# A fused transformer stack on one core: the last attention's token weights as a row, and a new order of steps

## The reference

```python
Sim = (x @ w1)[:, :, None] + (ctx @ w2)[:, None, :] + einsum('bid,bjd->bij', x * w3, ctx) + b_sim
A = softmax(Sim, axis=2)
hq_hat = einsum('bij,bjd->bid', A, ctx)
Batt = softmax(max(Sim, axis=2), axis=1)          # one weight per token
hc_bar = einsum('bi,bid->bd', Batt, x)[:, None, :]
feats = concatenate([x, hq_hat, x * hq_hat, x * hc_bar], axis=-1)
out = feats @ W_qv + b_qv
```

## Time and profile before

| | us |
|---|---|
| median of 3 runs (3061.4 to 3073.03) | 3064.12 |
| the profiled execution's own time | 3070.26 |
| its span | 3068.5 |

### The profile page before, as it was taken

How to read it: one execution, slowest core, us unless ns; L and a number is a source line. 1 busy time by engine, 2 the same in 40 slices (tenths; PEclk the granted TensorE clock), 3 DMA queues, 4 the chain that set the end, 5 groups by cost and what they waited for, 6 DMA issues and landing times. The chain is left out here.

```text
span 3068.5 us, 78311 instructions
## 1 busy us (share of the span) xinstructions
PE 2755.7 (90%) x28313; PEld 1958.0 (64%) x28313; DVE 2595.8 (85%) x6995; ACT 2420.2 (79%) x6105; POOL 1027.2 (33%) x1693
## 2 busy tenths in 40 slices
PE   6999999999999669979999997976799999999997
PEld 4666666666666446657777775332667777777776
DVE  5899999999999426459999995798499999999996
ACT  3899989999999435547777774498499999999995
POOL 1344444444444200035555552000034444444441
PEclk8999999999999679989999997998899999999998
DMA  1012121111111021101111110000300000000000
GB/s 49 27 34 62 51 38 34 35 34 35 34 34 33 14 61 43 42 21 35 34 34 34 34 35 25 12 0 0 105 9 16 16 16 16 16 16 16 16 16 9
DMA packets 177630, 91.15 MB, mean 30 GB/s; under 512 B 46339, under 2 KB 174021, under 8 KB 177251
## 3 DMA queue, kind: packets, MB, share of 16 engines
q1 hardware_dynamic: 171716, 76.85, 9.3%
q0 software_dynamic: 4096, 8.40, 0.8%
q10 hardware_dynamic: 1440, 0.90, 0.1%
HBM read 43.73 MB, written 42.36 MB: 28 GB/s over the span
## 5 line engine op out<-in xcount | busy, mean ns | idle before, releaser
L2336 DVE TENSOR_TENSOR th<-tf 128x2048 f32<-128x2048 f32 (+1 forms) x256 | 574.1, 2243 | 6.6 <-ACT cg L2139 6.6
L2168 ACT ACTIVATE th<-th 128x2048 f32<-128x2048 f32 (+1 forms) x256 | 481.6, 1883 | 0.6 <-DVE th L2336 0.6
L652 ACT ACTIVATE probf<-probf,colf 128x128 f32<-128x128 f32 x1024 | 313.2, 393 | 0.0
L2116 POOL TENSOR_SCALAR colf<-colf 128x1 f32<-128x1 f32 x64 | 134.8, 2107 | 441.0 <-DVE colf L2317 441.0
L2230 PE MATMUL p_rho<-th,late_w_row 128*32 128x128 f32 x8064 | 277.5, 276 | 2.5 <-ACT th L2168 2.3
L2230 PEld LDWEIGHTS p_rho<-th,late_w_row 128*32 128x32 f32 x8064 | 209.3, 110 | 26.7 <-ACT th L2168 3.6
L1765 PE MATMUL acc<-xnT_all,wT 128*128 128x512 f32 x384 | 181.3, 625 | 29.6 <-DVE tmax L1957 13.2
L2179 ACT ACTIVATE tl<-tf 128x128 f32<-128x128 f32 x640 | 199.6, 391 | 0.0
L656 ACT COPY probTf<-fp 128x1024 f32<-128x1024 f32 x128 | 129.5, 1012 | 45.7 <-PE fp L800 45.7
L800 PE MATMUL fp<-ident,probf 128*128 128x128 f32 x1024 | 142.4, 284 | 23.6 <-ACT ygf L659 20.5
L747 PE MATMUL xp<-ident,prob 128*77 128x128 f32 x1024 | 142.3, 283 | 20.8 <-DVE colc L993 19.4
(11 more groups left out here) (437 smaller groups left out, 8543.1 us busy)
## 6 DMA issues: line engine op xcount, KB each, us to landing
rows<-zeros SPq DMA_DIRECT2D x64, 256.0 KB, 2.4
cxT<-in_ctxT SPq DMA_DIRECT2D x128, 38.5 KB, 1.9
xb<-rows SPq DMA_DIRECT2D x67, 64.0 KB, 1.8
rows<-yb SPq DMA_DIRECT2D x67, 64.0 KB, 1.5
x<-in_x SPq DMA_DIRECT2D x64, 64.0 KB, 1.8
x_mid<-x SPq DMA_DIRECT2D x64, 64.0 KB, 1.5
z<-x_mid SPq DMA_DIRECT2D x64, 64.0 KB
x_next<-z SPq DMA_DIRECT2D x64, 64.0 KB, 1.5
```

Source lines behind the costliest of these rows:

```text
L652: last = nc.scalar.activation(scores, scores, ACT.Exp, bias=colf[s][:, 16 + HALF * hf + h:17 + HALF * hf + h])
L2168: nc.scalar.activation(b, b, ACT.Tanh).then_inc(act_done, ACT_L.did(f"t{c}.tanh", e))
L2336: nc.vector.tensor_tensor(th[i % NT][:, 0:shape[1], :], tf[s][:, CHUNK[n]:CHUNK[n + 1]].unsqueeze(2).to_broadcast(shape), tf[s][:, FEAT:FE ...
```

## The change

x2.p is now one row of 128 exponents on one partition, with their sum behind it; x2.M gives the negated maximum at once, so x2.Mb and x2.negM are gone. x2.hq spreads the row and its sum over all partitions with one product of a row of ones (128 + 1 columns), and the product with the context stays. x2.hc multiplies the spread weights with the transposed tokens on VectorE, scales by the reciprocal and sums along the row into column 24. x2.out moves to columns 384 to 511 of `p_o`. All four orders of the pass are new.

```diff
 ACT_C, new:
+    x2.exp@4 x1.PT@1 x2.P@4 x2.PT@4 f1.uqT@3 x2.p@4 x2.kT@4 x1.xT f2.xT@5 f1.tanh@2 x2.feat@4 x1.qkv x2.xT@3 f1.xT@1
+    x1.exp f1.uround@2
 DVE_C, new:
+    f1.scale@2 x2.norm@4 f1.round@2 f1.silu@3 f1.xq@2 f1.uamax@3 f1.uclip@3 f1.urec@3 x1.max@1 f1.uscale@3 x2.x@5
+    x2.max@4 x1.z x2.score@4 x1.stats f2.stats@5 x2.rden@4 f1.uq@3 f2.aggr@5 x1.rden@1 x1.aggr x1.x@1 f2.amax@8
+    f1.stats@1 x2.M@4 f1.aggr@1 f2.norm@5 x1.norm f1.x@3 x2.stats@3 f1.norm@1 x2.aggr@3 f1.amax@1 x2.rsum@4 f1.inv@1
+    x2.hc@4 x2.ehq@4
 PE_C, new:
+    f1.tap1@2 f1.down@3 f2.T@5 x2.hq@4 x1.T f1.z@2 x1.qkv x2.T@3 x2.out@4 x1.S f1.T@1 x2.S@3 x1.PT f1.tap0@1 x1.y
+    f1.uqT@2 x2.PT@3
 POOL_C, new:
+    x2.eps@5 x2.rstd@5 in.gather f2.eps@6 x1.eps@1 f2.rstd@6 x1.rstd@1 f1.eps@2 f1.rstd@2
...
+        p_row = ring(NC, "p_row", [1, TOK + 1])
+        spent = sb("spent", [128, TOK])
...
-                act.wait_ge(dve_done, DVE_M.value("x2.negM", e))
-                nc.scalar.activation(col[s][:, 22:23], col[s][:, 19:20], ACT.Exp, bias=col[s][:, 21:22])...
+                act.wait_ge(dve_done, DVE_M.value("x2.M", e))
+                nc.scalar.activation(p_row[s][0:1, 0:TOK], p_s[0:1, 384:512], ACT.Exp, bias=col[s][0:1, 20:21], accum_out=p_row[s][0:1, TOK:TOK + 1])...
...
-                    pe.wait_ge(dve_done, DVE_M.value("x2.negM", e - 1))
+                    pe.wait_ge(act_done, ACT_M.value("x2.p", e - 1))
...
-                pe.wait_ge(dve_done, DVE_M.value("x2.M", e))
-                nc.tensor.matmul(p_s[:, 208:209], ones[0:1, :], col[s][0:1, 20:21], start=True, stop=True)...
...
-                nc.tensor.matmul(p_o[:, 128:129], xn[s][:], col[s][:, 22:23], start=True, stop=True)
-                nc.tensor.matmul(p_o[:, 130:131], ones[:], col[s][:, 22:23], start=True, stop=True)
+                nc.tensor.matmul(p_o[:, 128:129 + TOK], ones[0:1, :], p_row[s][:], start=True, stop=True)
...
-                nc.vector.tensor_reduce(c[0:1, 20:21], p_s[0:1, 384:512], X_AXIS, ALU.max)...
-                dve.wait_ge(pe_done, PE_M.value("x2.Mb", e))
-                nc.vector.tensor_scalar(c[:, 21:22], p_s[:, 208:209], -1.0, None, ALU.mult)...
+                nc.vector.tensor_reduce(c[0:1, 20:21], p_s[0:1, 384:512], X_AXIS, ALU.max, negate=True)...
...
-                nc.vector.reciprocal(c[:, 23:24], p_o[:, 130:131])...
+                nc.vector.reciprocal(c[:, 23:24], p_o[:, 128 + TOK:129 + TOK])...
...
-                nc.vector.tensor_scalar(c[:, 24:25], p_o[:, 128:129], c[:, 23:24], None, ALU.mult)...
+                nc.vector.scalar_tensor_tensor(spent[:], p_o[:, 128:128 + TOK], c[:, 23:24], xnT[s][:], ALU.mult, ALU.mult, accum_out=c[:, 24:25])...
```

More of the change, by code:

```diff
@@ L169 @@
 F2_BEHIND = 3
+PE_C = """
+    f1.tap1@2 f1.down@3 f2.T@5 x2.hq@4 x1.T f1.z@2 x1.qkv x2.T@3 x2.out@4 x1.S f1.T@1 x2.S@3 x1.PT f1.tap0@1 x1.y
+    f1.uqT@2 x2.PT@3
+"""
 ACT_C = """
-    x2.xT@4 x1.exp@1 x2.feat@5 f1.uround@3 x1.PT@1 x2.exp@4 x2.P@4 f1.uqT@3 x2.PT@4 x1.xT f2.xT@5 f1.tanh@2 x2.p@4
-    x1.qkv f1.xT@1 x2.kT@4
+    x2.exp@4 x1.PT@1 x2.P@4 x2.PT@4 f1.uqT@3 x2.p@4 x2.kT@4 x1.xT f2.xT@5 f1.tanh@2 x2.feat@4 x1.qkv x2.xT@3 f1.xT@1
+    x1.exp f1.uround@2
 """
 DVE_C = """
[L175 to L182, removed]
+    f1.scale@2 x2.norm@4 f1.round@2 f1.silu@3 f1.xq@2 f1.uamax@3 f1.uclip@3 f1.urec@3 x1.max@1 f1.uscale@3 x2.x@5
+    x2.max@4 x1.z x2.score@4 x1.stats f2.stats@5 x2.rden@4 f1.uq@3 f2.aggr@5 x1.rden@1 x1.aggr x1.x@1 f2.amax@8
+    f1.stats@1 x2.M@4 f1.aggr@1 f2.norm@5 x1.norm f1.x@3 x2.stats@3 f1.norm@1 x2.aggr@3 f1.amax@1 x2.rsum@4 f1.inv@1
+    x2.hc@4 x2.ehq@4
 """
 POOL_C = """
-    x1.rstd@3 f2.eps@8 f2.rstd@8 f1.eps@4 f1.rstd@4 x2.eps@6 x2.rstd@6 in.gather x1.eps@2
+    x2.eps@5 x2.rstd@5 in.gather f2.eps@6 x1.eps@1 f2.rstd@6 x1.rstd@1 f1.eps@2 f1.rstd@2
 """
@@ L1270, in x2 @@
                 yield
-                act.wait_ge(dve_done, DVE_M.value("x2.negM", e))
-                nc.scalar.activation(col[s][:, 22:23], col[s][:, 19:20], ACT.Exp, bias=col[s][:, 21:22]).then_inc(act_done, ACT_M.did("x2.p", e))
+                act.wait_ge(dve_done, DVE_M.value("x2.M", e))
+                nc.scalar.activation(p_row[s][0:1, 0:TOK], p_s[0:1, 384:512], ACT.Exp, bias=col[s][0:1, 20:21], accum_out=p_row[s][0:1, TOK:TOK + 1]).then_inc(act_done, ACT_M.did("x2.p", e))
                 yield
@@ L1394, in x2 @@
                 yield
-                pe.wait_ge(dve_done, DVE_M.value("x2.M", e))
-                nc.tensor.matmul(p_s[:, 208:209], ones[0:1, :], col[s][0:1, 20:21], start=True, stop=True).then_inc(pe_done, PE_M.did("x2.Mb", e))
-                yield
                 pe.wait_ge(act_done, ACT_M.value("x2.p", e))
@@ L1408, in x2 @@
                 for n, f in enumerate((xnT, kT, qT, yT)):
-                    nc.tensor.matmul(p_o[:, 256:256 + DIM], f[s][:], w_qv2[:, n, :], start=(n == 0), stop=False)
-                nc.tensor.matmul(p_o[:, 256:256 + DIM], ones_bf[:], row_bq, start=False, stop=True).then_inc(pe_done, PE_M.did("x2.out", e))
+                    nc.tensor.matmul(p_o[:, 384:384 + DIM], f[s][:], w_qv2[:, n, :], start=(n == 0), stop=False)
+                nc.tensor.matmul(p_o[:, 384:384 + DIM], ones_bf[:], row_bq, start=False, stop=True).then_inc(pe_done, PE_M.did("x2.out", e))
                 yield
@@ L1540, in x2 @@
                 dve.wait_ge(act_done, ACT_M.value("x2.PT", e))
-                nc.vector.tensor_reduce(c[0:1, 20:21], p_s[0:1, 384:512], X_AXIS, ALU.max).then_inc(dve_done, DVE_M.did("x2.M", e))
-                yield
-                dve.wait_ge(pe_done, PE_M.value("x2.Mb", e))
-                nc.vector.tensor_scalar(c[:, 21:22], p_s[:, 208:209], -1.0, None, ALU.mult).then_inc(dve_done, DVE_M.did("x2.negM", e))
+                nc.vector.tensor_reduce(c[0:1, 20:21], p_s[0:1, 384:512], X_AXIS, ALU.max, negate=True).then_inc(dve_done, DVE_M.did("x2.M", e))
                 yield
                 dve.wait_ge(act_done, ACT_M.value("x2.kT", e))
-                nc.vector.reciprocal(c[:, 23:24], p_o[:, 130:131]).then_inc(dve_done, DVE_M.did("x2.rsum", e))
+                nc.vector.reciprocal(c[:, 23:24], p_o[:, 128 + TOK:129 + TOK]).then_inc(dve_done, DVE_M.did("x2.rsum", e))
                 yield
                 after("x2.rsum", e)
-                nc.vector.tensor_scalar(c[:, 24:25], p_o[:, 128:129], c[:, 23:24], None, ALU.mult).then_inc(dve_done, DVE_M.did("x2.hc", e))
+                if e >= 1:
+                    after("x2.hc", e - 1)
+                nc.vector.scalar_tensor_tensor(spent[:], p_o[:, 128:128 + TOK], c[:, 23:24], xnT[s][:], ALU.mult, ALU.mult, accum_out=c[:, 24:25]).then_inc(dve_done, DVE_M.did("x2.hc", e))
                 yield
@@ L1554, in x2 @@
                 dve.wait_ge(pe_done, PE_M.value("x2.out", e))
-                nc.vector.tensor_tensor(z[s][:], p_o[:, 256:256 + DIM], z[s][:], ALU.add).then_inc(dve_done, DVE_M.did("x2.x", e))
+                nc.vector.tensor_tensor(z[s][:], p_o[:, 384:384 + DIM], z[s][:], ALU.add).then_inc(dve_done, DVE_M.did("x2.x", e))
                 yield
```

## The result

| | us |
|---|---|
| before, median of 6 runs | 3068.95 |
| changed, median of 6 runs (3082.67 to 3095.91) | 3085.94 |
| ratio, 95% interval | 1.0055 [1.0043, 1.0067] |
| forecast | 3072, range 3035 to 3096 |

The change made the kernel slower by 17 us. The forecast was 8 us slower, on a median of 3064.12 from the three runs of before that were known then: its direction was right, its size half of it. In the profiled executions the span went from 3068.5 to 3084.7.

A forecast was written before the change was run, and what follows sets the result against it. VectorE was taken to bound, with waits on ScalarE and GpSimd lengthening the turn from 8.42 to 8.56 us: +8.8 us over 63 turns, less 1 at the run-out, so +8 on 3064.12 gives 3072; range 3035 to 3096.

The forecast's parts named there:

- What bounds: VectorE sets the pace in the old second pass, by its work plus about 0.11 us per dependent neighbouring pair; turn 8.42.
- The chain through ScalarE: Two exponents around f1.uround delay x2.rden to 3.51 us after f1.silu, against 3.24 by VectorE's list: a wait of 0.27.
- The chain through GpSimd: GpSimd's eps and rstd steps delay the three norms by 0.46 us together; f1.norm at 6.66, x2.norm at 8.11.
- The next f1.silu at 8.56: End of the walked turn: f1.silu follows f1.round at 8.36, so a turn is 8.56 us against 8.42, +0.14.
- TensorE gets between 0.1 and 1.2 us back: Per turn, three products go and one single-partition product comes, taken to hold 0.22; 0.4 us saved, counted as slack.
- VectorE's +0.06 for the mean: Longer weighted mean with sum read-out, less two removed VectorE steps: net +0.05 to +0.13 us a turn, free in its gap.
- The round trip at the run-out: Removed maximum round trip through VectorE, TensorE and ScalarE counts once, at the last entry: 1 us gained, between 0 and 3.
- B: Rival, chance 0.13: TensorE's clock falls if its idle stretch behind x2.S reaches about 1 us; +48 us, about 3115.
- C: Rival, chance 0.10: sum read-out and single-partition product each cost 0.1 us beyond the slack; turn 8.7, time 3080.
- D: Rival, chance 0.18: the order matters little, the waits wander and the turn stays at 8.42 us; time 3063.
- A: Rival: shorter waits on ScalarE and GpSimd; mild, chance 0.13, turn 8.15, 3046; full, chance 0.08, turn 7.75, 3021.
- the signs of being wrong: Turn under 8.3, clock below 1.00 in mid-pass, or the last TensorE product, not GpSimd, releasing x2.norm's neighbours.

The follow-up runs named there:

- e8: New computation in the four orders of before, weighted mean over only 8 of 128 tokens, against the kernel before: ratio 0.9995, turn 8.47 us.
- e3: Changed kernel with the row of weights and its ones in bf16, making the spreading product one pass instead of two: ratio to before 1.0001, turn 8.51 us.
- e2: Changed kernel with the spreading product of x2.hq issued twice into the same place: ratio to before 1.0136, turn 8.98 us.
- e6: Computation of before, with x2.Mb, x2.negM and the short mean, put in the changed kernel's new orders: ratio to before 1.0169, turn 9.26 us.
- e5: Changed kernel with the weighted mean over only 8 of the 128 tokens: ratio to before 1.0055, turn 8.76 us.
- e7: New computation in orders found by a search over a walk of all engines: 3051.19 against 3072.56 us for the kernel before, ratio 0.9935.

## Why the prediction came out as it did

The time lies in the stated range and on the side that was forecast, but part of that is luck. The turn, 8.77, lies outside the forecast's 8.48 to 8.64, and by the forecast's own chain, as the trace has it, it would have been near 8.53 (below). What made it longer was a chain that the forecast did not have.

**What bounds.** Right for the kernel before: e8 shows the old orders follow VectorE's work (0.11 a turn for the shortened mean). That a turn's length is VectorE's list plus its waits carried over; which wait ends last did not.

**The chain through ScalarE.** x2.rden 3.51 after f1.silu, by the sum; 1608.84 - 1605.31 = 3.53. Right.

**The chain through GpSimd.** f1.norm by the sum 6.66, measured 6.59; x2.norm 8.11, measured 8.01; f1.round 8.36, measured 8.33. The waits are there and shorter by up to 0.1, since steps of one kind in a row hold less than I took: two eps 0.37 in place of 0.44, two rstd 1.08 in place of 1.12. GpSimd's timeline has them merged:

```profile
1609.53 0.40 POOL L1187 TENSOR_SCALAR col<-col 128x1 f32<-128x1 f32 x2 [3.63 <-DVE col L1472]
1609.90 1.11 POOL L1190 TENSOR_TENSOR col<-col,minus_half 128x1 f32<-128x1 f32 x2
```

f1.round at 8.33 and 0.20 more give 8.53 for this chain alone; e3 has 8.51, with f1.tanh as late. The sum was 8.56.

**"The next f1.silu at 8.56."** This is the step that failed. f1.silu follows f1.round, and it also waits for f1.tanh. I had followed TensorE's work only as far as x2.M, called the rest slack, and had not walked x2.hq, f1.z and f1.tanh to f1.silu. That chain ends at 8.77. e2 and e3 show it from both sides: x2.hq 0.22 longer gave a turn 0.21 longer, and x2.hq 0.25 shorter gave one 0.26 shorter. e6 shows that what stands ahead of x2.hq is on it too. The part that I did walk held: x2.M near 5.05 by the sum, 5.06 measured (1610.37 - 1605.31).

**"TensorE gets between 0.1 and 1.2 us back."** The mis-sized term. x2.hq holds 0.74 in place of 0.67, and x2.Mb, which held 0.31 (1606.35 to 1606.66), is saved: 0.24 back, where I took 0.4. I took 0.22 for the single-partition product, with 0.54 as the upper end; it holds 0.41. At 0.22, x2.hq would be 0.19 shorter and the turn near 8.58, by my estimate from these rows: inside the forecast, though still by the chain that I had not walked.

**VectorE's +0.06 for the mean.** The row for the read-out was right: 0.08 long, and the next instruction starts with it (1613.04). The mean holds 0.28. In the new order it costs nothing, as said (e5). In the old one it costs about 0.1 (e8).

**The round trip at the run-out**, 1 us; the stretch behind the last x1.z is 0.6 shorter, with all that changed in it. I had said that in the steady part other entries cover it. e6 shows that they do not in this order: there it is worth 0.49 a turn.

**The rivals.** B, the clock, did not come: 1.00 through the stretch. TensorE's idle time before x1.PT is 0.33 and its busy share 94%, where I had said 0.7 to 0.9 and 80 to 90%; it had less room than I gave it. So B's condition, an idle stretch of about 1 us in mid-pass, was never met, and no run tests it. C came closest: its turn of 8.7 is 17 us more, which is what was measured. It named the right product, but as a cost beyond slack, with the forecast's chain still in charge. D's 8.42 was the wrong turn. A did not come in this order; e7 shows that a turn near 8.0, between its two forms, is there to be had in another. Of the signs of being wrong the last one came, in effect: TensorE's f1.z, through f1.tanh, and not GpSimd released f1.silu, two steps behind x2.norm.

## What to carry to other kernels

When the last thing an instruction waits for is on another engine, walk every chain that ends at it, not only the one through the engine that seems to bind; two chains here lay 0.24 us apart, and the one that was not walked set the time. A saved instruction is worth what the chain that ends last gives back: the same edit saved 0.49 us a turn in one order and cost 0.15 in another. Searched orders gained with either computation (0.4% and 0.7% of the whole time against the kernel before), though the walk behind them missed the turn by 0.1 to 0.3 us in two of three cases.

## What the runs showed that I had not expected

A product from a single partition is not as cheap as its columns. It holds TensorE 0.41 us where a 128-column product from 128 partitions, as part of x2.out in the same trace, holds 0.22:

```profile
1605.95 0.39 PE L1408 MATMUL p_io<-w_qv,kT 128*128 128x128 f32 x2
1606.17 0.39 PE L1408 MATMUL p_io<-w_qv,qT 128*128 128x128 f32 x2
```

Part of that is the change to it and back: issued twice it adds 0.23 (e2), and the context product behind it, from 77 partitions, holds 0.33. The weight loads show where it goes:

```profile
1611.32 0.29 PEld L1402 LDWEIGHTS p_io<-p_row,ones 1*128 1x128 f32 x2
1611.73 0.30 PEld L1403 LDWEIGHTS p_io<-probT,cx 77*128 77x128 f32 x2
...
1612.06 0.30 PEld L1367 LDWEIGHTS p_gv<-w_conv,xqT 128*128 128x128 f32 x2
```

For f1.z the load begins 0.11 ahead of the product, at 1612.06 for 1612.17, and the same holds within x2.out. For the single-partition product and for the one behind it load and product begin together, at 1611.32 and 1611.73, so here the first load is not hidden behind the product before. Of the two in e2 the second has its load 0.11 ahead again (1607.01 and 1607.12). Why the load is not hidden at the change was not tried.
